# Graph attention on dense score tiles: scores as float32 products of 64 rows in two halves of TensorE's array, ScalarE holding the lower bound of even tiles, and keys that the linear layer delivers already turned

## The chip, the cores and the metric

One Trainium2 chip, one of its cores. The metric is the device time of one execution of the whole program in microseconds (us), given as the median of several runs.

## The reference, cut to what matters

The program is a four-layer graph network over 6250 nodes (padded here to 49 tiles of 128, NT = 49) with 64 features and 200,000 edges. The change lies in the third layer, attention over the edges:

```python
qk = x @ qk_w.T + qk_b
v = x @ v_w.T + v_b
scores = jnp.sum(qk[dst] * qk[src], axis=-1) / math.sqrt(v.shape[-1])
scores = jnp.clip(scores, -5.0, 5.0)
...
e = jnp.exp(scores - seg_max[dst])
seg_sum = jax.ops.segment_sum(e, dst, num_segments=n)
attn = e / seg_sum[dst]
out = jax.ops.segment_sum(attn[:, None] * v[src], dst, num_segments=n)
out = out @ o_w.T + o_b
```

## The kernel before, in words

The layers run one after the other, and each phase is a block of instruction streams that all engines leave together. Two layers of edge-wise attention (`gat_edges`) fill the first three quarters. They also build a dense matrix of edge counts, `adj_scr`, in the chip's main memory (128 source rows by 128 destination columns a tile, bf16). The third layer uses it: instead of gathering edges it computes the scores of all pairs of nodes, bounds them, takes the exponential, and multiplies by the counts.

**`linear`, tag `qkv_lin` (line 184).** For each group of four node tiles TensorE turns the 128x64 features (L209), ScalarE copies them out of PSUM, and TensorE multiplies them by the 65x128 weights of keys and values (L218, the 65th row is the bias). VectorE copies the result into `qkv` (L244).

**`attention`, first block (from line 1302).** `split3` (L395 to L403) makes three bf16 parts of the keys on VectorE, whose sum is the float32 key. TensorE turns them in ten matmuls a tile (L1331) into `sides`, which holds for each tile five 128x128 bf16 arrangements of pairs of parts. VectorE (L1315) and ScalarE (L1321) copy them.

**`attention`, second block.** Destinations are taken in twelve groups g of GT = 4 tiles (512 columns) and a last group of one tile (128 columns). In a group, c runs over the 49 source tiles:
- TensorE, `scores`: three bf16 matmuls with 512 columns (L1380 to L1382) into the PSUM bank `at_s` number c % 4. The wait on `s_exp` says that ScalarE has read that bank.
- ScalarE: `exp(score / 8)` out of PSUM into `ex` (L1445). It waits for the score and for the weighing of the tile four before, whose slot of `ex` it takes.
- VectorE, `clip` (L1464): bounds `ex` between exp(-5) and exp(5) (LOW, HIGH). `weigh` (L1473): multiplies by the counts `at_adj` into `wt`, which has eight slots and one for the last tile. `weigh` of the tiles of a quad waits until `total` of the quad two before has read its slots (`s_quad`).
- TensorE, `total`: for the four tiles of a quad, float32 matmuls with the values into `at_v` (L1392, alternately the lower and the upper 64 columns of the array) and with ones into `at_d` (L1396, four sets of 32 columns).

The order is written out by hand. TensorE issues the scores of quad j, then `total` of quad j - 2. There are 13 quads to a group (NQD); the last one holds tile 48 alone. After the group's last total, two quads into the next group, ScalarE copies `at_v` and `at_d` out (`evacuate`, L1437, L1438), TensorE turns them back (`turn_back`, L1405, L1406) and VectorE divides (`finish`). SyncE loads the counts in seven pieces of seven tiles a group into four slots (L1363, 896 KB each), up to 22 tiles ahead of the weighing.

After `attention`, `linear` with tag `o_lin` and `add_pair` follow. Further on, `gcn_mlp` has a linear layer whose first product has 65 rows, 128 array columns and 512 moving columns (L1143).

Of the kernel before, what the change touches and what calls it, by code (L numbers as in the profile page):

```python
# [20 lines left out]
P = 128  # L21
N = 6250
D = 64
# [1255 lines left out]
def attention(nc, k, adj_d, qkv, out, ident, identb, ones):  # L1279
# [11 lines left out]
    AHEAD = 64  # L1291
    LOW, HIGH = float(np.exp(-5.0)), float(np.exp(5.0))

    s_set, s_tr, s_copied = k.sem("at_set"), [k.sem(f"at_turned{j}") for j in range(2)], [k.sem(f"at_copied{j}") for j in range(2)]
    s_in = [k.sem(f"at_in{j}") for j in range(SLOTS_IN)]
    s_score, s_exp, s_clip, s_weight, s_quad, s_evac, s_fold, s_out = (
        k.sem("at_" + n) for n in ("score", "exp", "clipped", "weight", "quad", "evac", "folded", "out"))
    with ExitStack() as own:
        sides = k.sb("at_sides", [P, NT, 5, P], BF16, own)
        fold = k.sb("at_fold", [P, D], F32, own)  # L1300
        pick = k.sb("at_pick", [P, 1], F32, own)
        with ExitStack() as prep:
            split = k.sb("at_split", [P, NT, 3, D], BF16, prep)
            turned = [k.ps(f"at_turned{j}", [P, 5, P], BF16, prep) for j in range(4)]
            block = prep.enter_context(nc.Block())

            @block.vector
            def _(dve):
                split3(dve, qkv[:, :, 0:D], lambda j: split[:, :, j, :], out[:])
                dve.tensor_tensor(fold[:], ident[:, 0:D], ident[:, D:P], ALU.add)  # L1310
                dve.tensor_reduce(pick[:], ident[:].rearrange("p (a b) -> p a b", b=32)[:, :, 0], AX.X, ALU.add)
                dve.drain().then_inc(s_set, 1)
                for t in range(0, NT, 2):
                    dve.wait_ge(s_tr[0], t // 2 + 1)
                    dve.tensor_copy(sides[:, t, :, :], turned[t % 4][:]).then_inc(s_copied[0], 1)  # L1315

            @block.scalar
            def _(act):
                for t in range(1, NT, 2):
                    act.wait_ge(s_tr[1], t // 2 + 1)  # L1320
                    act.activation(sides[:, t, :, :], turned[t % 4][:], ACT.Copy).then_inc(s_copied[1], 1)  # L1321

            @block.tensor
            def _(pe):
                pe.wait_ge(s_set, 1)
                for t in range(NT):
                    if t >= 4:
                        pe.wait_ge(s_copied[t % 2], t // 2 - 1)
# [3 lines left out]
                    last.then_inc(s_tr[t % 2], 1)  # L1332

# [18 lines left out]

        def quads_of(g, j):

            return g * NQD + (j + 1 + FREE)

        @block.sync
        def _(sp):
# [7 lines left out]
            with sp.Fori(0, GROUPS) as g:  # L1366
                group(g, GT)
# [3 lines left out]
        def _(pe):  # L1371
            pe.sem_inc(s_quad, FREE)

            def scores(g, j, tiles):
                for c in range(*quads[j]):
                    before = g * NT + (c - 3 if c >= 4 else c - 4 if c else 0)
                    pe.wait_ge(s_exp, before + FREE)
                    to = sps[c % 4][:, 0:tiles * P]
                    ask = lambda part: sides[:, bass.ds(g * GT, tiles), 2 + part, :]
                    pe.matmul(to, sides[:, c, 1, :], ask(2), start=True, stop=False)  # L1380
                    pe.matmul(to, sides[:, c, 0, :], ask(1), start=False, stop=False)
                    pe.matmul(to, sides[:, c, 0, :], ask(0), start=False, stop=True).then_inc(s_score, 1)  # L1382

            def total(g, j, tiles):
# [5 lines left out]
                for c in range(a, z):  # L1390
                    h = c % 2
                    pe.matmul(vps[h * D:h * D + D, 0:w], qkv[:, c, D:2 * D], wt[:, wt_slot(c), 0:w],  # L1392
                              start=(c < 2), stop=(c + 2 >= NT))
# [15 lines left out]
            def group(g, tiles, first=False):  # L1409
                for j in range(NQD):  # L1410
                    scores(g, j, tiles)
# [7 lines left out]
            group(0, GT, True)  # L1419
            with pe.Fori(1, GROUPS) as g:  # L1420
                group(g, GT)
            group(GROUPS, LAST)
# [5 lines left out]
        def _(act):  # L1428
            act.sem_inc(s_exp, FREE)
            act.sem_inc(s_evac, 1)  # L1430

# [7 lines left out]

            def group(g, tiles, first=False):  # L1440
                for c in range(NT):
                    w = tiles * P
                    act.wait_ge(s_score, g * NT + (c + 1))
                    act.wait_ge(s_weight, weights_of(g, c - 4 if 4 <= c < END else c - 5 if c < 4 else -1))
                    act.activation(ex[:, ex_slot(c), 0:w], sps[c % 4][:, 0:w], ACT.Exp, scale=1.0 / 8.0).then_inc(s_exp, 1)  # L1445
                    if c == 7 and not first:
# [302 lines left out]
```

## Time and profile before

| | us |
|---|---|
| median of 3 runs (lowest, highest) | 6561.05 (6558.09, 6562.64) |
| the profiled execution, its own time | 6555.38 |
| its span | 6553.5 |
| TensorE busy, share of the span | 5634.2 (86%) |
| TensorE weight load busy | 3858.0 (59%) |
| VectorE busy | 4266.8 (65%) |
| ScalarE busy | 2346.2 (36%) |
| GpSimd busy | 3061.3 (47%) |

The profile is of one execution. Busy shares are averages over phases with different limits, and so they don't say what bounds the phase of the change. Starts are in us from the start of the span. A matmul record lasts from its start until its last result is there, so consecutive records overlap, and the pace of TensorE is read from start to start. A float32 matmul leaves two records, each of one pass over the columns; a bf16 matmul leaves one.

### The profile page before, as it was taken

To read this page: it belongs to the slowest core of one execution; us is meant where nothing else is said; L and a number is where in the kernel's file an instruction comes from. 1 tells how busy PE (TensorE), PEld (TensorE's weight loads), DVE (VectorE), ACT (ScalarE), POOL (GpSimd) and SP (SyncE) were. 2 spreads that over 40 slices of the span, in tenths; PEclk is the share of its full clock that TensorE was granted. 3 is DMA by queue.
4 is the path that set the end of the run, shared out by engine and by line. 5 is a ranking of instruction groups with operands and counts; after the bars stand their busy time and mean duration, and the time that the engine had idled before them with its cause. 6 is when DMAs were issued, how large, how long until landed. Compare 5 with 4: busy or idle time off the path is not lost. (4 is left out here: it accounts for less than half of the span.)

```text
span 6553.5 us, 176947 instructions
## 1 busy us (share of the span) xinstructions
PE 5634.2 (86%) x42237; PEld 3858.0 (59%) x42238; DVE 4266.8 (65%) x13369; ACT 2346.2 (36%) x4950; POOL 3061.3 (47%) x3216
## 2 busy tenths in 40 slices
PE   0399999999999938999999999996785999994978
PEld 0366666666666626666666666664773333334978
DVE  5477777777777766777777777776326666665131
ACT  0144444444444414444444444442002444441000
POOL 0177777777777707777777777772000000000000
PEclk9999999999999959999999999997876999996979
DMA  1244444444444414444444444441741222222948
GB/s 47 55 113 106 107 107 109 107 108 107 107 107 108 110 29 109 107 109 107 107 108 108 108 107 107 109 106 36 309 172 40 90 95 90 84 81 104 379 183 308
DMA packets 706049, 768.34 MB, mean 117 GB/s; under 512 B 375941, under 2 KB 628909, under 8 KB 680885
## 3 DMA queue, kind: packets, MB, share of 16 engines
q1 hardware_dynamic: 584087, 583.69, 29.5%
q0 software_dynamic: 102400, 105.06, 8.5%
q10 hardware_dynamic: 19488, 78.68, 3.1%
q8 instruction: 37, 0.61, 0.0%
q14 instruction: 37, 0.30, 0.0%
HBM read 678.14 MB, written 88.81 MB: 117 GB/s over the span
## 5 line engine op out<-in xcount | busy, mean ns | idle before, releaser
L681 POOL DMA_INDIRECT gat_rows<-rows_scr,gat_idx x3200 | 3055.7, 955 | 1334.7 <-issue 1128.9
L727 DVE TENSOR_SCALAR adj_hot_key<-adj_iota_key,adj_winbase,adj_key 128x392 bf16<-128x392 int16 x2416 | 954.0, 395 | 0.0
L927 PE MATMUL gat_sps<-gat_relu,gat_att 128*128 128x256 f32 x3200 | 906.7, 406 | 0.0
L887 PE MATMUL gat_counts<-adj_hot_key,adj_hot_lo 128*128 128x392 bf16 x2416 | 748.0, 335 | 180.2 <-DVE adj_hot_key L727 66.9
L825 ACT ACTIVATE gat_weightsT<-gat_tps 128x512 f32<-128x512 f32 x800 | 477.7, 597 | 1173.0 <-PE gat_tps L937 1162.0
L811 ACT ACTIVATE gat_weights<-gat_masked,gat_newtop 128x512 f32<-128x512 f32 x800 | 577.5, 722 | 877.0 <-DVE gat_newtop L780 745.7
L726 DVE TENSOR_SCALAR adj_hot_lo<-adj_iota_lo,adj_low 128x128 bf16<-128x128 int16 x2416 | 677.4, 280 | 242.4 <-issue 223.3
L944 PE MATMUL gat_aps<-gat_rows,gat_weightsT 128*128 128x65 f32 x6400 | 803.5, 269 | 0.0
L944 PEld LDWEIGHTS gat_aps<-gat_rows,gat_weightsT 128*128 128x128 f32 x6400 | 777.8, 192 | 0.0
L887 PEld LDWEIGHTS gat_counts<-adj_hot_key,adj_hot_lo 128*128 128x128 bf16 x2416 | 232.5, 96 | 751.8 <-DVE adj_hot_key L727 556.3
L912 PE MATMUL gat_mps<-gat_ea,gat_we 128*128 128x256 f32 x1600 | 524.6, 410 | 159.8 <-DMA gat_rows<-rows_scr,gat_idx 147.0
L927 PEld LDWEIGHTS gat_sps<-gat_relu,gat_att 128*128 128x128 f32 x3200 | 543.4, 189 | 178.7 <-issue 137.3
L780 DVE CUSTOM_DVE_ANT_0 gat_masked<-gat_sps,gat_miss,gat_oldtop 128x512 f32<-128x512 f32 x800 | 597.4, 747 | 0.0
L1473 DVE TENSOR_TENSOR at_wt<-at_ex,at_adj 128x512 f32<-128x512 f32 (+1 forms) x637 | 416.0, 655 | 220.3 <-PE at_d L1396 218.0
L1445 ACT ACTIVATE at_ex<-at_s 128x512 f32<-128x512 f32 (+1 forms) x637 | 362.3, 573 | 485.1 <-DVE at_wt L1473 397.1
L1051 PE MATMUL gcn_sum_b<-gcn_parts,gcn_sum_adj 128*128 128x193 bf16 x4802 | 414.8, 249 | 102.7 <-DVEq L1083 102.7
L772 DVE COPY gat_oldtop<-gat_top 128x1 f32 x800 | 122.8, 154 | 562.4 <-issue 520.1
L937 PE MATMUL gat_tps<-ident,gat_weights 128*128 128x128 f32 x3200 | 483.1, 274 | 1.8
L919 PE MATMUL gat_mps<-ident,gat_rows 128*64 128x128 f32 x6400 | 483.6, 273 | 0.0
L1051 PEld LDWEIGHTS gcn_sum_b<-gcn_parts,gcn_sum_adj 128*128 128x128 bf16 x4802 | 413.9, 98 | 103.5 <-issue 103.0
L915 PE MATMUL gat_mps<-gat_hit,gat_xr 128*64 128x256 bf16 x4800 | 415.5, 281 | 0.0
L831 ACT ACTIVATE adj_tiles<-gat_counts 128x392 f32 (+1 forms) x784 | 385.7, 492 | 0.0
(320 smaller groups left out, 6969.5 us busy)
## 6 DMA issues: line engine op xcount, KB each, us to landing
gcn_sum_adj<-adj_scr SPq DMA_DIRECT2D x98, 1568.0 KB, 8.5
gat_dstb<-dst_scr SPq DMA_DIRECT2D x800, 128.0 KB
gat_ea<-in_ea SPq DMA_DIRECT2D x800, 128.0 KB
gin_sum_adj<-adj_scr SPq DMA_DIRECT2D x49, 1568.0 KB, 8.3
adj_scr<-adj_tiles ACTq DMA_DIRECT2D x48, 1568.0 KB
at_adj<-adj_scr SPq DMA_DIRECT2D x84, 896.0 KB, 4.8
gat_rows<-rows_scr,gat_idx POOLq DMA_INDIRECT x3200
gat_xr<-xr_scr SPq DMA_DIRECT2D x1600, 24.0 KB
```

The source lines that it names most:

```text
L681: pool.indirect_dma_start(rows[:, u, c, 0:ROW], None, rows_d, bass.IndirectOffsetOnAxis(ap=idx[:, u, c:c + 1], axis=0)).then_inc(s_g[u], 16)
L726: dve.tensor_scalar(plan.hot_lo[:, slot, :], plan.iota_lo[:], plan.low[:, bass.ds(c, 1)], None, ALU.is_equal)
L727: dve.tensor_scalar(plan.hot_key[:, slot, :], plan.iota_key[:], plan.winbase[:, bass.ds(w, 1)], plan.key[:, bass.ds(c, 1)], ALU.add, ALU.i ...
L780: dve.tensor_tensor_reduce(masked[:, j, :], sps[j][:], miss[:, o, :], 1.0, oldtop[:, o:o + 1], ALU.add, ALU.min, accum_out=newtop[:, j:j + ...
L811: act.activation(wts[:, j, :], masked[:, j, :], ACT.Exp, bias=newtop[:, j:j + 1], scale=-1.0)
L887: return pe.matmul(bank[:, 0:WD * NT], plan.hot_lo[:, slot, :], plan.hot_key[:, slot, :], start=start, stop=False)
L912: pe.matmul(mps[j][:, 0:GE // 2], we[:], ea[:, v, :], start=True, stop=False)
L919: last = pe.matmul(mps[j][64 * (c // 2):64 * (c // 2) + 64, P * (c % 2):P * (c % 2) + P], rows[:, v, c, 0:D], ident[:], start=False, stop= ...
L927: last = pe.matmul(sps[j][:, h * (GE // 2):(h + 1) * (GE // 2)], att[:, h, :], relu[:, j, :], start=True, stop=True)
L937: last = pe.transpose(tps[:, c * P:(c + 1) * P], wts[:, j, c * P:(c + 1) * P], ident[:])
L944: last = pe.matmul(aps[:, 0:D + 1], wtsT[:, j, c * P:(c + 1) * P], rows[:, v, c, 0:D + 1], start=(c == 0), stop=(c == GC - 1))
L1051: last = pe.matmul(banks[b % 2][:, 0:W], adj[:, b, hi * P:(hi + 1) * P], parts[:, hi, :], start=(hi == 0), stop=(hi == NT - 1))
```

## The change

It has three parts.

1. A new phase `keys_and_values` takes the place of `linear("qkv_lin")`. Per group of four tiles, one float32 matmul with the key weights, laid twice side by side, as the stationary side and the turned features as the moving side (65 rows, 512 columns) gives the keys already turned, and twice: features 0 to 63 on partitions 0 to 63 and again on 64 to 127. Four matmuls give the values in the usual layout. The first block of `attention` (three bf16 parts, turning, copies) is gone.
2. A score tile is one float32 matmul of 64 rows, 128 array columns and 512 columns: even tiles on partitions 0 to 63, odd tiles on 64 to 127. The destinations' keys are copied by SyncE's DMAs into two slots `ask`, each group's a group ahead; the DMA of group g waits until all scores of group g - 2 are made.
3. For even tiles (but for the last) ScalarE makes `relu(score / 8 + 5)` (`low`) and then, in a second instruction, `exp(. - 5)` (`late`), so that VectorE needs one instruction for the upper bound and the counts (`scalar_tensor_tensor`). Odd tiles and the last go as before. TensorE's waits for a free PSUM bank are on `s_low` or `s_exp` accordingly. The groups' loop on TensorE and SyncE takes two groups a turn.

```diff
+def keys_and_values(nc, k, h, w_d, keys, values, ident):
...
+                for t in range(a, z):
+                    op = pe.transpose(turned[g % 2][0:D, (t - a) * P:(t - a + 1) * P], h[:, t, :], ident[:])
...
+                pe.matmul(kp[g % 2][:, 0:n], wk[:].rearrange("p a f -> p (a f)"), ht[:, g % 2, 0:n],
+                          start=True, stop=True).then_inc(s_keys, 1)
+                for t in range(a, z):
+                    op = pe.matmul(vp[g % 2][:, (t - a) * D:(t - a + 1) * D], ht[:, g % 2, (t - a) * P:(t - a + 1) * P],
+                                   wv[:], start=True, stop=True)
...
+                dve.tensor_copy(keys[:, a:z, :].rearrange("p t n -> p (t n)"), kp[g % 2][:, 0:n]).then_inc(s_kout, 1)
...
-                split3(dve, qkv[:, :, 0:D], lambda j: split[:, :, j, :], out[:])
...
-                    for c, pair in enumerate(((0, 1), (2, 0), (0, 0), (1, 1), (0, 2))):
-                        for half, part in enumerate(pair):
-                            last = pe.transpose(turned[t % 4][half * D:half * D + D, c, :], split[:, t, part, :], identb[:])
...
+            def ask_next(g, slot):
+                sp.wait_ge(s_score, (g - 1) * NT)
+                sp.nop(nofuse=True)
+                sp.dma_start(ask[:, slot, :, :], keys[:, bass.ds(g * GT, GT), :]).then_inc(s_ask[slot], 16)
+
+            for slot in range(2):
+                sp.dma_start(ask[:, slot, :, :], keys[:, slot * GT:slot * GT + GT, :]).then_inc(s_ask[slot], 16)
+            group(0, GT)
+            with sp.Fori(0, GROUPS // 2 - 1) as i:
+                ask_next(i * 2 + 2, 0)
+                group(i * 2 + 1, GT)
+                ask_next(i * 2 + 3, 1)
+                group(i * 2 + 2, GT)
...
-                    before = g * NT + (c - 3 if c >= 4 else c - 4 if c else 0)
-                    pe.wait_ge(s_exp, before + FREE)
-                    to = sps[c % 4][:, 0:tiles * P]
-                    ask = lambda part: sides[:, bass.ds(g * GT, tiles), 2 + part, :]
-                    pe.matmul(to, sides[:, c, 1, :], ask(2), start=True, stop=False)
-                    pe.matmul(to, sides[:, c, 0, :], ask(1), start=False, stop=False)
-                    pe.matmul(to, sides[:, c, 0, :], ask(0), start=False, stop=True).then_inc(s_score, 1)
+                    if c % 4 in (0, 2) and c:
+                        pe.wait_ge(s_low, lows_of(g, c - 4))
+                    else:
+                        pe.wait_ge(s_exp, directs_of(g, c - 4 if c >= 4 else c - 6 if c else -1))
+                    rows = slice(c % 2 * D, c % 2 * D + D)
+                    pe.matmul(sps[c % 4][:, 0:tiles * P], keys[rows, c, :],
+                              ask[rows, odd, 0:tiles, :].rearrange("p a n -> p (a n)"),
+                              start=True, stop=True).then_inc(s_score, 1)
...
+            def low(g, c, w):
+                act.wait_ge(s_score, g * NT + (c + 1))
+                act.wait_ge(s_weight, weights_of(g, c - 4 if c >= 4 else c - 5))
+                act.activation(ex[:, ex_slot(c), 0:w], sps[c % 4][:, 0:w], ACT.Relu, bias=five[:], scale=1.0 / 8.0
+                               ).then_inc(s_low, 1)
+
+            def late(g, c, w):
+                act.wait_ge(s_low, lows_of(g, c))
+                act.activation(ex[:, ex_slot(c), 0:w], ex[:, ex_slot(c), 0:w], ACT.Exp, bias=minus[:]).then_inc(s_late, 1)
...
+                for c in range(0, END, 2):
+                    low(g, c, w)
+                    direct(g, c + 1, w)
+                    late(g, c, w)
+                    if c == 6 and not first:
                         evacuate(g - 1, GT)
+                direct(g, END, w)
...
+                    dve.wait_ge(s_late, g * PAIRS + (c // 2 + 1))
+                    dve.scalar_tensor_tensor(w, e, HIGH, a, ALU.min, ALU.mult).then_inc(s_weight, 1)
```

On TensorE, in the first group's steady part, the instructions of the scores of one quad and the total behind them stood so before (`at_s` is a score bank, `at_v` and `at_d` the sums):

```order
L1380 MATMUL at_s<-at_sides 128x512
L1381 MATMUL at_s<-at_sides 128x512
L1382 MATMUL at_s<-at_sides 128x512
L1392 MATMUL at_v<-at_wt,qkv 64x512 x4
L1396 MATMUL at_d<-at_wt,ones 32x512 x4
```

And so they stand in the change:

```order
L1453 MATMUL at_s<-at_ask,keys 128x512 x4
L1465 MATMUL at_v<-at_wt,values 64x512 x4
L1469 MATMUL at_d<-at_wt,ones 32x512 x4
```

The first three rows of before stand there once for each of the quad's four tiles, so twelve bf16 matmuls became four float32 ones; the totals and their place are the same.

On ScalarE the second block began with the load of a table and then one instruction a tile. Now it begins so (`at_five` and `at_minus` hold 5 and -5):

```order
L1527 ACTIVATE at_ex<-at_s,at_five 128x512
L1522 ACT_TABLE_LOAD
L1522 ACTIVATE at_ex<-at_s 128x512
L1532 ACTIVATE at_ex<-at_ex,at_minus 128x512
L1527 ACTIVATE at_ex<-at_s,at_five 128x512
L1522 ACTIVATE at_ex<-at_s 128x512
L1532 ACTIVATE at_ex<-at_ex,at_minus 128x512
```

Two tiles are three instructions, and the table is loaded once in the block, behind the first `low`.

On SyncE the second block now begins so:

```order
L1429 DMA at_ask<-keys 128x512 x2
L1420 DMA at_adj<-adj_scr 128x4x896 x7
L1431 UNCONDITIONAL_BRANCH
L1431 ISA
L1426 ISA
L1426 DMA at_ask<-keys 128x512
L1419 REGISTER_ALU
L1420 ISA
L1420 DMA at_adj<-adj_scr 128x4x896
```

Before, the queue held the loads of counts alone. Now two copies of keys are ahead of the first of them, and in each later group one copy, with its wait for the scores, is ahead of that group's seven.

## Rows read from the trace of the kernel before

**Rows 1.** Busy time by stretch: us, each engine's busy time, granted clock, DMA

```profile
5110.40:5181.70 71.30, 71.30 (x360) 23.14 (x359) 48.02 (x102) 30.13 (x52) 0.00 (x0) 1.00 0.29 91
...
5890.20:5913.10 22.90, 22.06 (x335) 15.76 (x333) 15.60 (x86) 11.92 (x43) 0.00 (x0) 1.00 0.12 33
6250.00:6290.00 40.00, 40.00 (x138) 29.21 (x137) 9.97 (x19) 5.97 (x10) 0.00 (x0) 0.50 0.00 0
```

**Rows 2.** Timeline of PE, one quad: start us, us, engine line op tiles xcount

```profile
5301.69 1.94 PE L1392 MATMUL at_v<-at_wt,qkv 128*64 128x512 f32 x8
5303.56 1.07 PE L1396 MATMUL at_d<-at_wt,ones 128*32 128x512 f32 x8
5304.56 0.39 PE L1380 MATMUL at_s<-at_sides 128*128 x1
...
5305.00 0.38 PE L1382 MATMUL at_s<-at_sides 128*128 x1
...
5307.25 1.94 PE L1392 MATMUL at_v<-at_wt,qkv 128*64 128x512 f32 x8
```

**Rows 3.** Timeline of PE, pieces of the same totals in narrow windows

```profile
5301.69 0.65 PE L1392 MATMUL at_v<-at_wt,qkv 128*64 128x512 f32 x2
...
5302.17 1.03 PE L1392 MATMUL at_v<-at_wt,qkv 128*64 128x512 f32 x4
...
5303.56 0.64 PE L1396 MATMUL at_d<-at_wt,ones 128*32 128x512 f32 x4
...
5304.01 0.61 PE L1396 MATMUL at_d<-at_wt,ones 128*32 128x512 f32 x4
```

**Rows 4.** Timeline of all engines in that quad, VectorE and ScalarE

```profile
5300.08 0.68 DVE L1473 TENSOR_TENSOR at_wt<-at_ex,at_adj 128x512 f32<-128x512 f32 x1
...
5300.68 0.42 DVE L1464 TENSOR_SCALAR at_ex<-at_ex 128x512 f32<-128x512 f32 x1
...
5301.02 0.68 DVE L1473 TENSOR_TENSOR at_wt<-at_ex,at_adj 128x512 f32<-128x512 f32 x1
...
5304.69 0.69 DVE L1473 TENSOR_TENSOR at_wt<-at_ex,at_adj 128x512 f32<-128x512 f32 x1 [1.72 <-PE at_d L1396]
...
5305.49 0.60 ACT L1445 ACTIVATE at_ex<-at_s 128x512 f32<-128x512 f32 x1 [2.23 <-PE at_s L1382]
```

**Rows 5.** Timeline of ACT where two groups end

```profile
5110.44 0.60 ACT L1437 ACTIVATE at_sums<-at_v 128x512 f32<-128x512 f32 x1 [1.38 <-PE at_d L1396]
5110.93 0.59 ACT L1438 ACTIVATE at_dens<-at_d 128x512 f32<-128x512 f32 x1
...
5181.68 0.60 ACT L1437 ACTIVATE at_sums<-at_v 128x512 f32<-128x512 f32 x1 [1.39 <-PE at_d L1396]
```

**Rows 6.** Timeline of DVE in an earlier layer, two kinds of instruction

```profile
4934.65 3.42 DVE L1260 SCALAR_TENSOR_TENSOR z_sb<-z_sb,h_sb 128x3136 f32<-128x3136 f32 x1
4938.15 3.42 DVE L1262 TENSOR_TENSOR x_sb<-x_sb,z_sb 128x3136 f32<-128x3136 f32 x1
```

**Rows 7.** Timeline of all engines, from the end of the linear layer on

```profile
4995.83 0.89 DVE L244 COPY qkv<-qkv_lin_mp 128x512 f32<-128x512 f32 x2 [1.23 <-PE qkv_lin_mp L218]
...
4997.96 1.82 DVE L395 CAST at_split<-qkv 128x3136 bf16<-128x3136 f32 x1 [1.24 <-PEq L86]
...
5033.48 11.86 SPq L1363 DMA_DIRECT2D at_adj<-adj_scr  x5
...
5038.49 0.69 DVE L1473 TENSOR_TENSOR at_wt<-at_ex,at_adj 128x512 f32<-128x512 f32 x1 [2.28 <-DMA at_adj<-adj_scr]
```

**Rows 8.** Timeline of PE, steady groups of two linear layers

```profile
4966.36 1.91 PE L218 MATMUL qkv_lin_mp<-qkv_lin_w_sb,qkv_lin_ht_sb 65*128 65x128 f32 x8
...
4968.92 1.91 PE L218 MATMUL qkv_lin_mp<-qkv_lin_w_sb,qkv_lin_ht_sb 65*128 65x128 f32 x8
...
6257.32 1.91 PE L1143 MATMUL gcn_mlp_hp<-gcn_mlp_ht_sb,gcn_mlp_wa 65*128 65x512 f32 x2
...
6261.48 1.92 PE L1143 MATMUL gcn_mlp_hp<-gcn_mlp_ht_sb,gcn_mlp_wa 65*128 65x512 f32 x2
```

More of the change, by code:

```diff
@@ L1281, in attention @@
+@phase
+def attention(nc, k, adj_d, keys, values, out, ident, ones):
     GT = 4
@@ L1298, in attention @@
     with ExitStack() as own:
-        sides = k.sb("at_sides", [P, NT, 5, P], BF16, own)
         fold = k.sb("at_fold", [P, D], F32, own)
         pick = k.sb("at_pick", [P, 1], F32, own)
[L1302 to L1308, printed above, removed]
-                split3(dve, qkv[:, :, 0:D], lambda j: split[:, :, j, :], out[:])
[L1310 to L1328, printed above, removed]
-                    for c, pair in enumerate(((0, 1), (2, 0), (0, 0), (1, 1), (0, 2))):
-                        for half, part in enumerate(pair):
-                            last = pe.transpose(turned[t % 4][half * D:half * D + D, c, :], split[:, t, part, :], identb[:])
-                    last.then_inc(s_tr[t % 2], 1)
+        five = k.sb("at_five", [P, 1], F32, own)
+        minus = k.sb("at_minus", [P, 1], F32, own)
+        ask = k.sb("at_ask", [P, 2, GT, P], F32, own)
         adj = k.sb("at_adj", [P, SLOTS_IN, GT, PIECE * P], BF16, own)
@@ L1391, in total @@
                     h = c % 2
[L1392 removed]
+                    pe.matmul(vps[h * D:h * D + D, 0:w], values[:, c, :], wt[:, wt_slot(c), 0:w],
                               start=(c < 2), stop=(c + 2 >= NT))
@@ L1407, in turn_back, with group @@
                 last.then_inc(s_fold, 1)
-            def group(g, tiles, first=False):
+            def group(g, turn, tiles, odd, first=False):
+                pe.wait_ge(s_ask[odd], turn * 16 + 16)
+                pe.nop(nofuse=True)
                 for j in range(NQD):
-                    scores(g, j, tiles)
+                    scores(g, j, tiles, odd)
                     if j >= 2:
@@ L1417, in group @@
                         turn_back(g - 1, GT)
[L1419 to L1422, printed above, removed]
+            group(0, 0, GT, 0, True)
+            with pe.Fori(0, GROUPS // 2 - 1) as i:
+                group(i * 2 + 1, i, GT, 1)
+                group(i * 2 + 2, i + 1, GT, 0)
+            group(GROUPS - 1, GROUPS // 2 - 1, GT, 1)
+            group(GROUPS, GROUPS // 2, LAST, 0)
             total(GROUPS, NQD - 2, LAST)
@@ L1486, in group @@
             def group(g, tiles, first=False):
-                clip(g, 0, tiles * P)
-                for c in range(1, NT):
-                    clip(g, c, tiles * P)
-                    weigh(g, c - 1, tiles)
+                for c in range(0, END, 2):
+                    clip(g, c + 1, tiles * P)
+                    weigh(g, c, tiles)
+                    if c == END - 2:
+                        clip(g, END, tiles * P)
+                    weigh(g, c + 1, tiles)
                     if c == 20 and not first:
@@ L1640, in build @@
         with ExitStack() as own:
-            qkv = node("qkv", own, 2 * D)
-            linear(nc, k, "qkv_lin", h, ins["w_qkv"], 2 * D, qkv, ident)
-            attention(nc, k, adj_d, qkv, z, ident, identb, ones)
-            linear(nc, k, "o_lin", z, ins["w_o"], D, qkv, ident)
-            add_pair(nc, k, z, qkv, h)
+            keys = k.sb("keys", [P, NT, P], F32, own)
+            values = node("values", own)
+            keys_and_values(nc, k, h, ins["w_qkv"], keys, values, ident)
+            attention(nc, k, adj_d, keys, values, z, ident, ones)
+            linear(nc, k, "o_lin", z, ins["w_o"], D, values, ident)
+            add_pair(nc, k, z, values, h)
         norm("at_ln", z, z)
```

108 lines of the change are left out of this document (91 added, 17 removed).

## The prediction

> **What bounds the kernel now.** The change touches the third layer alone, so I read that stretch and not the page's shares. Busy time by stretch comes first [rows 1]: in a full group of attention TensorE is busy all of its 71.3 us at a granted clock of 1.00 (2.4 GHz), VectorE 48.0 and ScalarE 30.1. The timeline says that this is work and no artefact of overlapping records [rows 2]: a quad (scores of four tiles, total of an older quad) repeats every 5307.25 - 5301.69 = 5.56 us. Its parts, start to start: values 1.87 (5301.69 to 5303.56), ones 1.00 (to 5304.56), scores 2.69 (to 5307.25; twelve bf16 matmuls at 0.22, 5304.56 to 5305.00 being two, and the lead-in of the next kind). VectorE needs 0.60 + 0.34 = 0.94 a tile, from the start of one weighing over the clip to the next [rows 4], 3.76 a quad, and idles 1.72 until TensorE's total frees its slots, as the bracket of the row at 5304.69 says. So TensorE is the limit, and a group's period, from one evacuation to the next, is 5181.68 - 5110.44 = 71.24 us [rows 5]: twelve quads of 5.56 and 4.52 for tile 48 and the turning back.
>
> **How float32 matmuls of parts of the array run.** What the scores will cost hangs on this. A float32 matmul of 512 columns leaves two records. In the values' total the first records of two matmuls (lower and upper columns) start together at 5301.69 (x2), the next two at 5302.17, and the stretch of 1.03 with x4 holds one more pair, 1.03 - 0.60 = 0.43 later. With four sets of columns the four first records start at 5303.56 and the four second ones at 5304.01 [rows 3]. So a pass takes 0.43, a matmul two passes, and matmuls in different parts of the array share the time. A second pass begun at 5304.01 would let the next kind start at 5304.44; it starts at 5304.56, a lead-in of 0.1. The first pass of a total took 0.48, about 0.05 more than 0.43, since its weights (64 columns) aren't loaded ahead; with 128 columns I estimate 0.10. Parts by rows are nowhere in this trace: that is the unknown.
>
> **The steady part.** Removed per quad: twelve bf16 matmuls. Added: four float32 matmuls, two in each half of the rows. If the halves share time as the columns' do, this is four pairs of passes: 4 x 0.43 + 0.10 + 0.09 lead-in = 1.91 instead of 2.69. The quad takes 1.91 + 1.87 + 1.00 = 4.78, that is 0.78 less. Tile 48 has no partner: 0.10 + 0.86 + 0.09 = 1.05 instead of 0.74, 0.31 more. A group gains 12 x 0.78 - 0.31 = 9.05 and has a period of 62.2. Bounds for the scores of a quad: below, 1.72 with nothing before it; above, all eight passes in a row, 3.62. I take 1.91, since the values' total, the nearest row, does four matmuls of the same size in two parts in 1.87.
>
> **Does anything else take over as the limit?** Set the start of a quad's scores to 0. Scores 0 and 1 are there at 1.12 (0.53 for the first pass, 0.59 for the second record), scores 2 and 3 at 1.98. ScalarE starts 0.11 after a score (5305.00 + 0.38 = 5305.38 to 5305.49) [rows 2, 4], and its instructions of 512 columns follow each other by 0.49 [rows 5]. The six of a quad start at 1.23, 1.72, 2.21, 2.70, 3.19, 3.68 and end at 4.3. The banks that the next scores need at 4.78 are read at 3.8. ScalarE has 1 us to spare. VectorE: a pair is 0.34 + 0.60 + 0.60 = 1.54, if the fused instruction costs what the multiplication does, as it does in an earlier layer (3.42 and 3.42 for 3136 columns) [rows 6]. Per quad that is 3.08 (before 3.76), from 0.13 to 3.3, with the four weighings done at 0.8, 1.4, 2.4 and 3.0, each before ScalarE needs its slot. It then waits some 1.6 for the total. So the slack is less than before for ScalarE, but TensorE stays the limit, and VectorE's saved clips are worth nothing. They are hidden behind TensorE's total, and would count only if a quad fell under 3.1. The relu needs no other table: the order has one load in the block, behind the first `low`.
>
> **The queue of SyncE.** Each group's copy of keys stands ahead of its counts, and waits until the scores of the group before are all made. Before, the first counts were asked for some 15 tiles ahead. Now they are asked for at about 1.2 after tile 48's scores start. The scores of tile 0 are there 3.97 + 1.12 = 5.1 after that start, its `late` ends at 6.7, and only then is it weighed. A load lands 5.0 after its issue (5033.48 to 5038.49) [rows 7], so at 6.3, or 7.3 with the copy of 256 KB ahead. That is at most 0.6 late, and the quad's total is not due until two quads later. I cost it at nothing; its cover is 2 to 3 us wide, and if it failed it would cost up to 1 us in each of 12 groups.
>
> **Setup.** Removed: from the end of the linear layer's last copy at 4996.72 to the first weighing at 5038.49 is 41.8 us [rows 7]; it holds the three parts, the turning and the first load of counts. Now there remain 1.4 to the first issue (an estimate from the 1.24 in the bracket at 4997.96, the pause between two blocks), two copies of keys ahead in the queue (0.3 each to issue; their 512 KB beside the counts' 896 KB, 1.0), and 5.0 until the counts land: 8.0. Bounds: 7.0 if the copies cost nothing, 11 if they move as slowly as the counts and the table's load comes late. Saved: 33.8. The first group's first two quads of scores lay before the first weighing already, so their 2 x 0.78 = 1.6 are not to be counted again.
>
> Added in the new phase: the key matmul has 512 columns at the granted clock of 0.50 (1.2 GHz) that `gcn_mlp` shows (the last row) [rows 1]. `gcn_mlp` has this very sequence (four turnings, 65 rows by 512 columns, four matmuls of 64 columns) and repeats every 6261.48 - 6257.32 = 4.16, where `qkv_lin` repeats every 2.56 [rows 8]. 12 x 1.60, and 0.4 for the last tile and 0.6 for two more loads of weights: +20.2. VectorE's two copies hide behind the 4.16: two copies of 512 columns and less took 0.89 together [rows 7].
>
> **The last group** has 128 columns and took 22.9 us. ScalarE's chain gets longer there, VectorE's shorter, scores about equal: 0, between -3 and +4.
>
> **Sum.** 12 x 9.05 - 1.6 = 107.0 saved, 33.8 saved, 20.2 added: 120.6 less. The profiled execution, whose own time is 6555.4 (span 6553.5), would become 6434.8. It lies 5.7 under the median of the runs shown, 6561.05, so the forecast for the median is 6440.
>
> **Rivals.**
> 1. *Passes in program order.* The wait and the signal on each score keep the second matmul from overtaking the first one's second pass, so only second and next first passes share time: five pass times in a quad instead of four, 0.10 + 5 x 0.43 + 0.09 = 2.34. The quad takes 5.21 and a group gains 12 x 0.35 - 0.31 = 3.9: 12 x 3.9 - 0.7 + 33.8 - 20.2 = 60 less, 6501. Against it: the totals overtake [rows 3]; for it: they have no waits between them, and here there is one each. The Trainium skill ("TensorE: Matmul & The Clock Gate", Part 3) says that matmuls start and end strictly in program order. By that rule the quad would be this rival's; the trace disagrees, for in rows 3 four first records stand ahead of four second ones.
> 2. *The halves do not share time (slower).* Both halves of the rows write all 128 partitions of a bank, where the totals' parts each write their own; if TensorE runs them one after the other, a quad's scores are eight passes, 3.62, and the quad 6.49. A group loses 12 x 0.93 + 0.31 = 11.5, and with the first group's correction 136 in all; less 33.8, plus 20.2: 122 more, 6683. It decides from a score phase of 2.69 on in the steady part, and from 2.75 on in the sum (13.6 from the setup is 0.09 a quad). For it: nothing in the trace shows parts by rows. Against it: a float32 pass gives a column only every second cycle (512 in 0.43), so two halves write no faster than one bf16 matmul (512 in 0.22) does [rows 2, 3].
>
>    The Trainium skill ("TensorE: Matmul & The Clock Gate", Part 3) gives 3.07 times the speed for matmuls of 32 rows and 512 columns in four row parts of the array. By that figure the halves would share time, as in my forecast; no row here shows it.
> 3. *ScalarE or the hand-overs become the limit.* Three instructions a pair and a chain of score, low, late, weigh. It needs 0.8 us an instruction instead of 0.49. At 5.1 a quad the time is 6440 + 147 x 0.32 = 6487. Against it: the rows leave 1 us.
>
> **How the numbers follow.** Forecast 0.70; rival 1 0.12; rival 2 0.11; rival 3 0.07. The range: down to 6420, if the 0.10 of first weights costs nothing (-14) and setup goes well (-3 to -5); up to 6505, to hold rivals 1 and 3. Outside are rival 2 and a little of the tails. The runs of this kernel tell apart about 0.2%, 13 us; all but rival 2 are faster by more: faster 0.88, same 0.01, slower 0.11.
>
> **What would show it.** In the new profile: the period from evacuation to evacuation at 62.2; the first records of two scores starting within 0.1 of each other; values to values 4.78; VectorE still waiting for `at_d`; no wait of weighing for `at_adj` but the first; 4.16 a group in the new phase at clock 0.50; some 8 us from its last copy to the first weighing. It would be wrong if score records start 0.43 apart with none together (rival 2), if only unlike passes overlap (rival 1), or if TensorE waits for ScalarE at the scores (rival 3).

## The result and the profile after

| | before | after |
|---|---|---|
| median of the runs | 6559.57 us (6548.07 to 6562.64) | 6442.1 us (6428.76 to 6447.89) |
| ratio | | 0.9821, 95% interval 0.9802 to 0.9841 |
| profiled execution, its span | 6555.4, 6553.5 us | 6447.89, 6445.9 us |
| period of a full group of attention | 71.24 us | 62.28 us |
| third layer, first turning of its linear layer to the first of `o_lin` | 952.7 us (4963.87 to 5916.59) | 835.1 us (4973.06 to 5808.14) |

The kernel is 117 us faster; the forecast was 6440. I take the third layer's own length as the sharp measure from here on. It begins between 4961 and 4976 us after the start in eleven of the thirteen profiles, and that wandering is in the whole time but not in the layer. In the other two (the first version with sums on VectorE and the last with sums on GpSimd, below) it begins near 6480 and 6459: beside them the kernel before took some 8070 us too, why is not known (chip 15 has both 6565 and 8080 us for it), and such runs are compared by the period and the layer alone.

Busy time by stretch (us, busy time of PE, PEld, DVE, ACT, POOL, granted clock, DMA share, GB/s): the new phase, a full group, the last group. These answer to [rows 1].

```profile
4973.00:5026.00 53.00, 51.37 (x173) 37.08 (x173) 14.67 (x27) 7.38 (x13) 0.00 (x0) 0.50 0.01 1
5100.50:5162.80 62.30, 62.30 (x314) 18.48 (x312) 40.11 (x78) 43.13 (x77) 0.00 (x0) 1.00 0.33 111
5782.50:5804.70 22.20, 21.46 (x294) 14.98 (x294) 13.13 (x65) 16.54 (x64) 0.00 (x0) 1.00 0.12 33
```

TensorE is still busy for the whole of a group. ScalarE went from 30.1 to 43.1 us in a group that is 9 us shorter, and VectorE from 48.0 to 40.1. Now the timeline of TensorE over one quad, as in [rows 2]:

```profile
5291.44 1.99 PE L1453 MATMUL at_s<-at_ask,keys 64*128 64x512 f32 x8
5293.36 1.94 PE L1465 MATMUL at_v<-at_wt,values 128*64 128x512 f32 x8
5295.23 1.06 PE L1469 MATMUL at_d<-at_wt,ones 128*32 128x512 f32 x8
5296.22 0.43 PE L1478 MATMUL at_f<-at_fold,at_sums 128*128 128x64 f32 x2
```

The start-to-start steps are 1.92 for the scores (5291.44 to 5293.36), 1.87 for the values, 0.99 for the ones: 4.78. Which records make up the 1.92 shows in narrow windows, as in [rows 3]:

```profile
5291.44 0.70 PE L1453 MATMUL at_s<-at_ask,keys 64*128 64x512 f32 x2
...
5291.97 1.02 PE L1453 MATMUL at_s<-at_ask,keys 64*128 64x512 f32 x4
...
5292.40 1.02 PE L1453 MATMUL at_s<-at_ask,keys 64*128 64x512 f32 x4
```

Two records start together at 5291.44, two at 5291.97, two at 5292.40, and the last two 0.43 later (each window of 1.02 is 0.43 + 0.59, one record's length). That is one pair of passes each time, four pairs in all; the first step is 0.53, the others 0.43. ScalarE and VectorE in the same quad, to be laid beside [rows 4]:

```profile
5291.67 0.69 DVE L1581 SCALAR_TENSOR_TENSOR at_wt<-at_ex,at_adj 128x512 f32<-128x512 f32 x1 [1.70 <-PE at_d L1469]
5292.27 0.68 DVE L1578 TENSOR_TENSOR at_wt<-at_ex,at_adj 128x512 f32<-128x512 f32 x1
5292.88 0.42 DVE L1564 TENSOR_SCALAR at_ex<-at_ex 128x512 f32<-128x512 f32 x1
```

```profile
5292.68 0.69 ACT L1527 ACTIVATE at_ex<-at_s,at_five 128x512 f32<-128x512 f32 x1 [0.89 <-PE at_s L1453]
5293.27 0.59 ACT L1522 ACTIVATE at_ex<-at_s 128x512 f32<-128x512 f32 x1
5293.74 0.72 ACT L1532 ACTIVATE at_ex<-at_ex,at_minus 128x512 f32<-128x512 f32 x1
5294.36 0.69 ACT L1527 ACTIVATE at_ex<-at_s,at_five 128x512 f32<-128x512 f32 x1
...
5295.40 0.73 ACT L1532 ACTIVATE at_ex<-at_ex,at_minus 128x512 f32<-128x512 f32 x1
```

VectorE idles 1.70 for TensorE's ones before each quad's first weighing, as it did before (1.72). ScalarE idles 0.89 for TensorE's scores, where it idled 2.23; a quad's six instructions take it 3.45 us (5292.68 to 5296.13). In the waits from 5027 to 5805 (total, times, longest) these are the two largest; no wait of weighing for the counts is long:

```profile
DVE at_wt L1581 <- PE at_d L1469: 193.4, 128, 2.1
ACT at_ex L1527 <- PE at_s L1453: 184.8, 124, 10.6
...
DVE at_wt L1581 <- DMA at_adj<-adj_scr: 4.8, 8, 1.0
```

The start of attention, to be laid beside [rows 7]:

```profile
5025.92 0.23 DVE L1351 COPY values<-kv_vp 128x64 f32<-128x64 f32 x1
5027.55 1.67 SPq L1429 DMA_DIRECT2D at_ask<-keys  x2
...
5029.27 2.50 SPq L1420 DMA_DIRECT2D at_adj<-adj_scr  x4
5030.49 7.15 PE L1453 MATMUL at_s<-at_ask,keys 64*128 64x512 f32 x15 [4.60 <-DMA at_ask<-keys]
5032.62 0.69 ACT L1527 ACTIVATE at_ex<-at_s,at_five 128x512 f32<-128x512 f32 x1 [10.59 <-PE at_s L1453]
5033.32 1.28 ACT L1522 ACT_TABLE_LOAD   x1
...
5035.96 0.69 DVE L1581 SCALAR_TENSOR_TENSOR at_wt<-at_ex,at_adj 128x512 f32<-128x512 f32 x1 [0.28 <-ACT at_ex L1532]
```

From the last copy's end (5026.15) to the first weighing it takes 9.8 us instead of 41.8. The first weighing waits for ScalarE, not for the counts: the chain is the copy of the keys, the first scores, `low`, the table's load, `direct`, `late`. The first scores run at half the clock (window of 5.30 us, as above):

```profile
5030.40:5035.70 5.30, 5.21 (x11) 2.33 (x12) 0.43 (x1) 3.05 (x4) 0.00 (x0) 0.50 1.00 347
```

In the kernel before the granted clock was 1.00 from 5019.8 on, ahead of its first weighing.

### The profile page after: what moved, and what is told of

Same layout as the page of the kernel before. It is cut to its first block and busy times, and to the rows that moved or that the text cites. A ratio compares the mean times of both kernels' runs of the same rounds, so it can differ in the third digit from the quotient of the medians.

```text
span 6445.9 us, 174609 instructions
## 1 busy us (share of the span) xinstructions
PE 5538.0 (86%) x41136; PEld 3798.8 (59%) x41137; DVE 4148.9 (64%) x13042; ACT 2493.4 (39%) x5238; POOL 3065.7 (48%) x3216
## 3 DMA queue, kind: packets, MB, share of 16 engines
q1 hardware_dynamic: 586115, 586.92, 30.1%
## 5 line engine op out<-in xcount | busy, mean ns | idle before, releaser
L919 PEld LDWEIGHTS gat_mps<-ident,gat_rows 128*64 128x64 f32 x6400 | 375.8, 137 | 0.1
L820 ACT ACTIVATE gat_relu<-gat_mps 128x256 f32<-128x256 f32 x800 | 307.4, 384 | 142.3 <-issue 124.7
```

Source lines behind the costliest of these rows:

```text
L919: last = pe.matmul(mps[j][64 * (c // 2):64 * (c // 2) + 64, P * (c % 2):P * (c % 2) + P], rows[:, v, c, 0:D], ident[:], start=False, stop= ...
```

## The experiments

The theory: TensorE's queue is the only limit of a group, and its scores are short because the two halves of the rows share the time. Rivals that a match of the total alone doesn't exclude: that the queue would have been shorter still without the signal on each score; that part of the 9 us came from VectorE's saved clips; that the copy of keys costs something at each group.

**One half for all scores.** The same matmuls, all in the lower half of the array's rows.

```diff
-                    rows = slice(c % 2 * D, c % 2 * D + D)
+                    rows = slice(0, D)
```

> All scores use rows 0 to 63; the keys stand on both halves, so nothing else changes. My theory (the two halves share time): the eight passes of a quad's scores now stand in a row, 4 x 0.43 = 1.72 more a quad, the period from evacuation to evacuation 62.28 + 12 x 1.72 = 82.9 us, the whole about 240 us longer, 6685. Rival (the gain comes from fewer instructions or from the float32 form itself, not from sharing): period near 62.3.

Measured: 6716.87 us (one run; the kernel before took 6563.38 beside it), third layer 1101.2 us. The timeline of TensorE:

```profile
5245.49 3.70 PE L1453 MATMUL at_s<-at_ask,keys 64*128 64x512 f32 x8
5249.12 1.94 PE L1465 MATMUL at_v<-at_wt,values 128*64 128x512 f32 x8
5250.99 1.06 PE L1469 MATMUL at_d<-at_wt,ones 128*32 128x512 f32 x8
5251.99 3.70 PE L1453 MATMUL at_s<-at_ask,keys 64*128 64x512 f32 x8
```

The quad is 6.50 (5245.49 to 5251.99) and the scores 3.63, against 3.62 as worked out for eight passes in a row. So the sharing of the two halves carries 1.71 us of each quad: without it the change would have been a loss. Most periods were 82.80, but three groups took 86.14. There the granted clock fell to 0.50 for 6.8 us while TensorE was busy without a pause, and rose again:

```profile
5130.00:5148.00 18.00, 18.00 (x72) 6.97 (x71) 8.60 (x16) 9.59 (x17) 0.00 (x0) 1.00 0.20 55
5148.00:5154.80 6.80, 6.80 (x13) 1.75 (x11) 0.43 (x1) 3.40 (x6) 0.00 (x0) 0.50 0.34 127
5154.80:5161.00 6.20, 6.20 (x24) 2.06 (x24) 3.17 (x6) 3.38 (x6) 0.00 (x0) 1.00 0.00 0
```

The three groups explain 10 of the 32 us by which the run lies over the expectation. Some 9 more lie in the first group, where the clock rose to 1.00 only at 5055.8 (5035.8 in the changed kernel), and 3 in the last. Why the clock fell I did not test.

**One signal a quad, and with it another choice of halves.** The first leaves only a quad's last score with a signal; the second also puts tiles 0 and 1 of a quad in the lower half and 2 and 3 in the upper, so that a tile's partner stands two places behind it.

```diff
-                              start=True, stop=True).then_inc(s_score, 1)
+                              start=True, stop=True)
+                    if c == quads[j][1] - 1:
+                        last.then_inc(s_score, quads[j][1] - quads[j][0])
```

```diff
-                    rows = slice(c % 2 * D, c % 2 * D + D)
+                    rows = slice(c // 2 % 2 * D, c // 2 % 2 * D + D)
```

> The signal of the scores comes once a quad, with the last of its four matmuls, instead of with each. My theory: ScalarE starts at 2.1 instead of 1.23 after the scores' start and ends at about 5.5, still before the next quad needs it; period 62.3. Rival (ScalarE has no such slack, rival 3 of the prediction): TensorE waits for the banks, period 64 to 70.

> As the run with one signal a quad, and the tiles c % 4 = 0 and 1 use the lower rows, 2 and 3 the upper ones, so that the partner of a matmul stands two places behind it. If each half of the array has a queue of its own: scores still 1.91, period as in that run, 62.3. If matmuls start strictly in program order, only one of eight passes has a partner: seven pass times, 1.29 more a quad, period 77.7, about 180 us more in all.

Measured: 6465.34 and 6465.21 us (one run each), third layer 851.1 and 852.9. Neither keeps the expected period of 62.3. The steady quad stays at 4.78 in both, so the signal on each score costs TensorE nothing. The period rises to 63.14 and 63.22, all of it in the quads about tile 48 and the next group's start. Ten periods are some 9 of the 16 and 18 us by which the layer is longer; another 4.5 to 5.4 are in the first group, where the clock rose to 1.00 for good at 5049.5 and 5046.0 instead of 5035.8. ScalarE gets a quad's scores later; in the list of waits from 5100 to 5700 TensorE's weight loads wait for ScalarE's reading of the banks 82.1 us in the first, against 25.2 in the changed kernel. With the partner two places behind, the first pass of tile 2 still starts beside that of tile 0 (PE, a window of 0.15 us):

```profile
5291.00 0.71 PE L1453 MATMUL at_s<-at_ask,keys 64*128 64x512 f32 x2
```

The two records start 13 ns apart, while tile 1, which stands between them in the program, starts only when tile 0 is through. So the halves behave as two queues of their own. In strict program order only tile 1's second pass could have shared with tile 2's first: seven steps of 0.43 instead of four.

**Clips.** ScalarE's lower bound and the fused instruction undone, the rest as changed; and the other way round, this part alone on the kernel before.

```diff
-                for c in range(0, END, 2):
-                    low(g, c, w)
-                    direct(g, c + 1, w)
-                    late(g, c, w)
+                for c in range(NT):
...
+                    act.activation(ex[:, ex_slot(c), 0:w], sps[c % 4][:, 0:w], ACT.Exp, scale=1.0 / 8.0).then_inc(s_exp, 1)
...
-                for c in range(0, END, 2):
-                    clip(g, c + 1, tiles * P)
-                    weigh(g, c, tiles)
...
+                clip(g, 0, tiles * P)
+                for c in range(1, NT):
+                    clip(g, c, tiles * P)
+                    weigh(g, c - 1, tiles)
```

> The third part of the change alone is undone: ScalarE makes one exponential a tile, VectorE clips and weighs every tile, as before. My theory (TensorE is the limit, the clips saved are hidden): period 62.3 still, time within 3 us of the change, VectorE's wait for the ones falls from about 1.7 to about 1.0 a quad. Rival (the chain score, exp, clip, weigh is too long for a quad of 4.78): 0.2 us or more a quad, period 64.7 or more, 30 us or more in all.

> The kernel before with one part of the change alone: the lower bound of even tiles on ScalarE (relu of the scaled score plus 5, then exp of that minus 5) and the fused upper bound and multiplication on VectorE; scores stay three bf16 products, the setup and the linear layer stay. Theory (TensorE limits both kernels, VectorE's clips were hidden): the period of a group stays 71.24 us, VectorE's busy time in a group falls from 48.0 to about 40 and ScalarE's rises from 30 to about 43, VectorE waits longer for TensorE's ones, the time stays at that of before within 0.2%. Rival (VectorE's work was part of the limit): a quad falls below 5.56 us and the time by more than 13 us. If ScalarE's three instructions a pair held up the scores, the period would be above 71.24.

Measured: undone, 6445.08 us, ratio to before 0.982 (0.9803 to 0.9836), period 62.28, third layer 834.4; added to the kernel before, 6559.52 us, ratio 1.0001 (0.9992 to 1.0011), period 71.24. A full group of each:

```profile
5100.50:5162.80 62.30, 62.30 (x312) 18.46 (x310) 48.00 (x102) 29.16 (x53) 0.00 (x0) 1.00 0.32 108
```

```profile
5184.70:5256.00 71.30, 71.30 (x360) 23.16 (x359) 40.27 (x78) 43.86 (x76) 0.00 (x0) 1.00 0.28 90
```

VectorE's busy time moves between 48.0 and 40.3 and the period doesn't move. This part of the change is worth nothing by itself in either kernel.

**The copy of keys behind the counts.**

```diff
-                ask_next(i * 2 + 2, 0)
                 group(i * 2 + 1, GT)
-                ask_next(i * 2 + 3, 1)
+                ask_next(i * 2 + 2, 0)
                 group(i * 2 + 2, GT)
+                ask_next(i * 2 + 3, 1)
```

> The changed kernel with SyncE's copy of the next group's turned keys moved behind that group's loads of counts instead of ahead of them. Nothing else differs. Theory: the period of a group stays 62.28 us; VectorE's waits for the counts (4.8 us in all over 8 groups) go to about nothing, TensorE does not notice, the time is that of the changed kernel within 0.2%. Rival (the copy's place costs at the group boundary): the period falls by up to 1 us, the time by up to 12 us. If the keys come late instead, TensorE waits for them at each group's first score and the period rises.

Measured: 6436.62 us (6430.45 to 6443.85), ratio to before 0.9815 (0.9798 to 0.9831), period 62.28, third layer 834.7. The waits of weighing for the counts are gone from the list, and nothing else changed. The place in the queue costs 0, as its cover of 2 to 3 us said, though the prediction's sign for it, no such wait but the first, was not met: there were the 8 in the list above, 4.8 us in all.

**Sums of pairs on GpSimd.** A try to shorten what does limit: six of the twelve stretches of ones.

```diff
+                if j % 2:
+                    for p in range(2 * j - 2, 2 * j + 2):
+                        h = p % 4
+                        last = pe.matmul(dps[32 * h:32 * h + 32, 0:w], ones[:, 0:32], su[:, p % 8, 0:w],
...
+            def group(g, w):
+                for p in range(PAIRS):
...
+                    pool.tensor_tensor(su[:, p % 8, 0:w], wt[:, wt_slot(2 * p), 0:w], wt[:, wt_slot(2 * p + 1), 0:w],
+                                       ALU.add).then_inc(s_sum, 1)
```

> The changed kernel, but GpSimd adds the weights of two neighbouring tiles (128x512 float32, 24 additions a group) and TensorE multiplies ones by four such sums every second quad instead of by four tiles every quad; tile 48 alone as before. The sums of weights are taken in another order, nothing is left out. Theory (TensorE is the only limit): six stretches of ones of 1.00 us fall away in a group, the period goes from 62.28 to 56.3 us, the time falls by some 72 us to 6370. Two ways in which it fails: GpSimd needs over 2.2 us for an addition (two a quad of 4.4 us), then the quad becomes two additions long; or its additions slow VectorE's instructions, so that VectorE's 0.60 and 0.34 us in the records grow and it becomes the limit; either makes the period longer than 56.3 and, if over 62.28, the kernel slower than the changed one.

Measured: 6479.52 us (6476.98 to 6485.92), ratio to before 0.9885 (0.9868 to 0.9901), period 64.5 (two of ten 66.2): slower than the changed kernel, where 6370 was expected. In this version the values wait for the sums too. GpSimd's addition takes 1.37 and would fit. The timelines of POOL and DVE:

```profile
5227.26 1.39 POOL L1563 TENSOR_TENSOR at_su<-at_wt 128x512 f32<-128x512 f32 x1 [3.55 <-DVE at_wt L1598]
```

```profile
5225.89 0.69 DVE L1601 SCALAR_TENSOR_TENSOR at_wt<-at_ex,at_adj 128x512 f32<-128x512 f32 x1 [0.18 <-ACT at_ex L1539]
...
5226.50 0.68 DVE L1598 TENSOR_TENSOR at_wt<-at_ex,at_adj 128x512 f32<-128x512 f32 x1
...
5227.10 0.42 DVE L1584 TENSOR_SCALAR at_ex<-at_ex 128x512 f32<-128x512 f32 x1
...
5227.56 1.63 DVE L1601 SCALAR_TENSOR_TENSOR at_wt<-at_ex,at_adj 128x512 f32<-128x512 f32 x1
```

The weighing that starts at 5227.56 beside the addition ends at 5229.19, 0.54 after the addition's end at 5228.65. The one at 5225.89, with GpSimd idle, took 0.69. The clip at 5227.10 kept its 0.42. Of 203 fused weighings between 5150 and 5700, 177 start during an addition and have a median of 1.755, and each ends 0.55 after the addition does, wherever in it it began: it stands still until then. The 26 others have 0.679. VectorE needs 5.24 a quad and is the limit. Whether this lies in the fused instruction was the question of one more run: the same with a clip and a plain multiplication for each tile.

> The version with sums of pairs on GpSimd, and VectorE as in the version that clips every tile: no fused instruction, one clip and one plain multiplication a tile. In the version with fused instructions these took 1.75 us beside an addition of GpSimd and 0.68 without, while plain multiplications were hardly ever beside one and clips were and kept their 0.42. Theory A (an instruction of VectorE that reads two tiles waits until GpSimd's addition is over, whatever its kind): plain multiplications that fall beside an addition take up to 1.75 too, VectorE's quad is about 3.76 + 2 x 1.07 = 5.9, the period some 75 us, the third layer about 990 us, slower than the kernel before. Theory B (only the fused instruction suffers): multiplications keep 0.68, the period is 56.3 to 58.

Measured: 8074.36 us beside 8079.59 of the kernel before (one run each; the mean granted clock of the run is 0.88 instead of 0.94). Periods of 72.6 and 74.2 by turns, third layer 974.9, a little under the 75 and 990 of theory A. The timeline of DVE:

```profile
6899.84 0.41 DVE L1565 TENSOR_SCALAR at_ex<-at_ex 128x512 f32<-128x512 f32 x1
6900.18 1.76 DVE L1577 TENSOR_TENSOR at_wt<-at_ex,at_adj 128x512 f32<-128x512 f32 x1
6901.86 0.41 DVE L1565 TENSOR_SCALAR at_ex<-at_ex 128x512 f32<-128x512 f32 x1
6902.20 0.68 DVE L1577 TENSOR_TENSOR at_wt<-at_ex,at_adj 128x512 f32<-128x512 f32 x1
```

The plain multiplication suffers in the same way: 180 of 400 start during an addition and have a median of 1.75, the others 0.68. The clip is not spared either. The clips that kept their 0.42 beside an addition had all started before it. Of the 212 clips in the same stretch of the first version with GpSimd, 24 started during one; they took up to 1.49 and ended 0.28 to 0.34 after it. DVE and POOL there:

```profile
5151.31 1.28 DVE L1598 TENSOR_TENSOR at_wt<-at_ex,at_adj 128x512 f32<-128x512 f32 x2
5152.52 1.48 DVE L1584 TENSOR_SCALAR at_ex<-at_ex 128x512 f32<-128x512 f32 x1
```

```profile
5152.07 1.65 POOL L1563 TENSOR_TENSOR at_su<-at_wt 128x512 f32<-128x512 f32 x1 [1.57 <-DVE at_wt L1598]
```

The second of the two multiplications was running when the addition started, and kept its time; the addition took 1.65, where it takes 1.27 when VectorE is idle at its start and 1.38 when it starts during a clip. So neither the fused form nor the number of tiles read decides here who loses, but which of the two started first. The Trainium skill ("SBUF — State Buffer", Who interferes with whom) says that an instruction of VectorE with two inputs in SBUF contends with an instruction of GpSimd that reads SBUF, and that the order of issue decides which of them is blocked. The traces agree with both: 1.75 against 0.68 for a multiplication that comes second, and 0.68 for the 9 plain ones of the first version that came first.

**Sums of pairs on VectorE.** Its slack of 1.7 a quad holds two additions of 0.60.

```diff
+            def add(g, p, w):
+                dve.wait_ge(s_weight, weights_of(g, 2 * p + 1))
+                dve.tensor_tensor(su[:, p % 8, 0:w], wt[:, wt_slot(2 * p), 0:w], wt[:, wt_slot(2 * p + 1), 0:w],
+                                  ALU.add).then_inc(s_sum, 1)
...
                     clip(g, c + 1, tiles * P)
+                    if c:
+                        add(g, c // 2 - 1, tiles * P)
                     weigh(g, c, tiles)
```

> As the kernel with sums of pairs on GpSimd, but VectorE makes the sums itself, each one pair later, between a clip and a weighing; TensorE multiplies ones by four sums every second quad. The values no longer wait for sums. Theory (TensorE's work is the limit, VectorE has 1.6 us of slack a quad): VectorE's quad grows from 3.08 by two additions of 0.60 to 4.28, TensorE's falls to 3.78 and 4.78 by turns, 4.28 on average, so both are even; the period is 56.3 us if the slots even out the turns and up to 58 if not, the time 6370 to 6390. Rival (the short quads wait for VectorE, the long ones give nothing back): each pair of quads takes 4.78 + 4.28, the period 59.3, the time 6406. GpSimd is idle here: if VectorE's fused instruction takes 0.69 again where it took 1.54 to 1.76 beside an addition on GpSimd, that was what made the version with GpSimd slow.

> The version in which VectorE adds the weights of two tiles and TensorE multiplies ones by four sums every second quad, with the copy of the next group's turned keys behind the loads of counts too. Its predecessor had a period of 56.94 us on a chip on which all kernels are slower in the layers before, where TensorE's clock and the loads are lower than here. Expected: the period is 56.9 us again, the third layer takes 771 us against 835 of the changed kernel, the time is 64 us under the changed kernel's on the same chip: 6375 to 6380 where the kernel before takes 6560, ratio 0.972. If the sums hid a cost elsewhere, the difference to the changed kernel would be less than 60 us.

> The changed kernel again, beside the version with sums of pairs on the same chip, for a fair difference between the two. Expected: ratio to the kernel before 0.982, period 62.28 us.

Measured: the first took 7891.3 us beside 8062.04 of the kernel before, ratio 0.9789 (0.9766 to 0.9812), period 56.94, third layer 771.6. With the keys' copy behind the counts, on one chip with the changed kernel: **6384.45 us** (6380.15 to 6385.97), ratio to before **0.9723** (0.971 to 0.9736), and the changed kernel 6448.19, ratio 0.9823 (0.9808 to 0.9838). Period 56.94 against 62.28, third layer 771.6 against 834.6. The whole is 4 us over the upper end of what was expected, 6380; the difference of 64 us to the changed kernel is as expected. A stretch of some ten groups, with VectorE's groups of instructions (count, busy, mean ns, idle before):

```profile
5100.00:5700.00 600.00, 600.00 (x2768) 190.92 (x2764) 564.68 (x1065) 463.33 (x789) 0.00 (x0) 1.00 0.36 116
```

```profile
L1583 DVE TENSOR_TENSOR at_wt<-at_ex,at_adj 128x512 f32<-128x512 f32 x208 | 141.2, 682 | 0.0
L1586 DVE SCALAR_TENSOR_TENSOR at_wt<-at_ex,at_adj 128x512 f32<-128x512 f32 x201 | 137.5, 684 | 14.3 <-PE at_d L1472 6.9 <-PE at_v L1466 4.2 <-DMA at_adj<-adj_scr 1.2
L1590 DVE TENSOR_TENSOR at_su<-at_wt 128x512 f32<-128x512 f32 x201 | 137.0, 682 | 0.0
```

The fused weighing is at 684 ns again, VectorE is busy for 564.68 of 600 us, and TensorE still has no gap: TensorE is the limit, with VectorE close behind. Of the 0.66 over 56.28 that a group takes, 0.64 is one quad a group that follows its neighbour by 4.42 instead of 3.78. This version beats both kernels. It is also where the change's third part earns its place by arithmetic: without the saved clips VectorE's quad would be 3.76 + 1.20 = 4.96, more than the 4.28 of TensorE. That was not run.

## Why the prediction was right

- **What bounds.** TensorE before and after. Shown by the clip runs (VectorE's 8 us a group are worth 0) and by the runs in which TensorE's own work was changed: 20.5 us a group with one half for all, 5.34 with half the ones.
- **The scores of a quad.** Forecast 1.91, measured 1.92; the quad 4.78 and 4.78; the pair of passes at 0.43 as in the values' total, and 0.53 for the first, so the estimate of 0.10 for the first weights held. The rule of program order weighed in rival 1 would have given 5.21; the trace and the run with the partner two places behind disagree with it. Rival 2's price was right too (3.63 for 3.62), only its condition wasn't met.
- **The groups.** Period 62.28 for 62.2 (8.96 gained for 9.05). From the first weighing to the last full group's evacuation the time fell from 851.7 (5038.49 to 5890.23) to 746.6 (5035.96 to 5782.52): 105.2 for 107.0.
- **The new phase.** From its first turning to its last copy 53.1 instead of 32.9: 20.2 for 20.2. It repeats every 4.16 at a clock of 0.50 (1.2 GHz), as `gcn_mlp` did [rows 8].
- **The setup.** 32.0 saved for 33.8; this term was mis-sized. "Two copies of keys (0.3 each to issue)" took 1.67 together, and the load of counts was taken for the last link, while in truth it was the chain of keys, scores and ScalarE with its table. The first scores took 2.1 (5030.49 to `low` at 5032.62) instead of the 1.23 of the steady part, at a granted clock of 0.50. The 9.8 lies within the 11 us of the upper bound.
- **The last group.** 22.17 for 22.90, 0.7 saved where 0 was said.
- **Sum.** 105.2 + 32.0 + 0.7 - 20.2 = 117.7 less; the layer's own length says 117.6, the forecast 120.6. The two profiled executions differ by 107.5: the stretch before the layer happened to be 9.2 longer and the one behind it 0.9. The medians differ by 117.5. That the median came within 2 us of 6440 is partly luck: the sum saves 3 us too much, the base it starts from, 6561.05, lies 1.5 over the median of the comparison, and runs of one kernel differ by some 20 us. Only the scores and the clips have runs of their own; that the 32.0 and the 20.2 belong to the setup and the new phase is read from the two profiles.
- **ScalarE.** Forecast to end 4.3 after the quad's first score, measured 4.69 (5291.44 to 5296.13). `low` and `late` cost more than the evacuation of [rows 5]: a pair takes 1.68 (5292.68 to 5294.36, the next `low`) instead of 1.47. The 1 us of slack was enough; with the signal once a quad it was not, and the period rose by 0.86.
- **VectorE.** The fused instruction costs what the multiplication does (0.69 and 0.68), as [rows 6] said.

## What to carry to other kernels

Read the shape of one repeated step from start to start on the engine that never pauses: it gives the price of a replaced operation to a hundredth, and it tells that relief of any other engine is worth nothing, as long as the others keep their slack (one late signal a quad used up ScalarE's). An operation in a new shape can often be priced from records of the same kind elsewhere in the trace, here two records per float32 matmul that start together. When the limit has moved down far enough, spend the slack of the second engine on the first one's work, but on that engine itself: here the helper whose additions and VectorE's work hold each other up took more than it gave.

## What the runs showed of the hardware

- Float32 matmuls in the two halves of the rows start 6 ns apart and share all their time, although both write all 128 partitions of a bank: 1.92 us for four, 3.63 in one half. Each half takes its matmuls in order, but one half runs ahead of the other in the program.
- ScalarE's instruction of 128x512 takes 0.60 as an exponential from PSUM, 0.69 as a relu from PSUM with a bias tile, and 0.72 to 0.79 as an exponential from SBUF with a bias tile. No run separates function, source and bias.
- While GpSimd adds two SBUF tiles, a multiplication of two SBUF tiles on VectorE that starts during the addition stands still (1.75 instead of 0.68), and so does a clip in place (up to 1.49 instead of 0.42). Either keeps its time when it started first, and then the addition is the longer one (1.38 and 1.65 instead of 1.27).
- The granted clock fell to 0.50 for 6.8 us in three groups of the run with one half for all, with TensorE busy throughout. In both versions with GpSimd it fell to 0.50 for 3 to 7 us at a time, as here in the first (5218.5 and 5542.7 lie in the two periods of 66.2); in the changed kernel it stayed at 1.00 from 5035.9 to 5800.

```profile
5218.50:5221.90 3.40, 3.40 (x12) 0.58 (x14) 3.40 (x6) 0.56 (x1) 1.29 (x1) 0.50 1.00 348
```
